# Biases of the first experts added by VectorE, turned rows copied a quad ahead, mask rows loaded by group, two scatters a step in the last group

## The reference

```python
x = layernorm(x + state_space_layer(x))
# first experts: 8 experts of hidden size 512, the best 2 for each token
out = 0.5 * gelu(flat @ shared_W + shared_b)
for e in range(8):
    h = gelu(flat @ W1[e] + b1[e])
    out = out + combine[:, e:e+1] * (h @ W2[e] + b2[e])
x = layernorm(x + layernorm(out) * gamma + beta)
# causal attention, 16 heads of size 8
x = layernorm(x + (softmax(mask(q k^T / sqrt(8))) v) @ Wo + bo)
# second experts: 64 experts, the best 4 for each token, 128 slots for each expert
x = layernorm(x + routed(x, router_w, w1, w2))
```

## Time and profile before

| what | value |
|---|---|
| median of three runs | 1650.65 us (1644.73 to 1650.91) |
| the profiled execution | 1646.96 us, its span 1645.1 us |
| busy share PE, DVE, ACT, POOL | 81%, 73%, 56%, 57% |
| mean granted clock of TensorE | 0.892 of full speed |
| first experts, projections, attention with routing | 259, 38 and 607 us |

### The profile page before, as it was taken

One profiled execution on the slowest core, in us unless ns is written; L12 is line 12 of the kernel. 1 busy time (PEld: TensorE's weight loads), 2 busy tenths in 40 slices (PEclk: granted clock), 3 DMA queues, 4 the chain that ended last, 5 costly groups with the idle time before them and its releaser, 6 DMA issues. The chain is left out here.

```text
span 1645.1 us, 25186 instructions
## 1 busy us (share of the span) xinstructions
PE 1332.7 (81%) x7232; PEld 716.4 (44%) x7235; DVE 1200.2 (73%) x2215; ACT 916.3 (56%) x1728; POOL 943.3 (57%) x779
## 2 busy tenths in 40 slices
PE   6848888888888989999926999999999998812756
PEld 2313333333333358898913244443343343212743
DVE  6999999999999554224477988889889886260325
ACT  5746666665666554456555076675666566601423
POOL 2478899988998117360756021214563654874773
PEclk9879899999999988999957599999999999955867
DMA  2019100000000025787728211211321114301317
GB/s 70 0 59 345 56 0 0 0 0 0 0 0 0 1 61 141 205 240 199 208 55 256 60 32 37 56 31 31 83 55 35 50 35 106 60 10 47 106 51 257
DMA packets 123041, 124.87 MB, mean 76 GB/s; under 512 B 31182, under 2 KB 97979, under 8 KB 120304
## 3 DMA queue, kind: packets, MB, share of 16 engines
q1 hardware_dynamic: 101032, 99.70, 21.8%
q0 software_dynamic: 10240, 15.79, 3.3%
q10 hardware_dynamic: 11656, 8.00, 1.6%
HBM read 78.52 MB, written 50.91 MB: 79 GB/s over the span
## 5 line engine op out<-in xcount | busy, mean ns | idle before, releaser
L2106 DVE TENSOR_REDUCE t_negm<-t_ps 128x1 f32<-128x512 f32 (+4 forms) x624 | 370.0, 642 | 56.7 <-PE t_ps L2374 35.2
L2083 ACT ACTIVATE t_PT<-t_ps_s 128x1024 f32<-128x1024 f32 (+3 forms) x384 | 292.1, 811 | 203.6 <-PE t_ps_s L2393 202.6
L493 POOL TENSOR_TENSOR s_HC<-s_H,X 128x1024 f32<-128x1024 f32 x128 | 307.0, 2416 | 40.3 <-DVE s_H L614 30.1
L658 PE MATMUL ps_y<-s_HC,ident 128*128 128x512 f32 x512 | 270.5, 655 | 19.8 <-POOL s_HC L493 17.9
L2011 POOL TENSOR_SCALAR_AFFINE_SELECT t_PT<-t_PT 128x512 f32<-128x512 f32 x128 | 82.7, 646 | 276.7 <-ACT t_PT L2083 276.2
L2374 PE MATMUL t_ps<-heads 96*128 96x512 bf16 (+3 forms) x640 | 201.3, 341 | 9.4 <-DVE t_negm L2106 7.6
L2393 PE MATMUL t_ps_s<-heads 96*128 96x512 bf16 (+3 forms) x768 | 181.0, 329 | 3.7 <-ACT t_PT L2083 2.1
L2408 PE MATMUL t_ps_c<-t_PT,t_VG 128*32 128x512 f32 (+3 forms) x1536 | 164.7, 502 | 1.7 <-ACT t_CT L2039 1.1
L554 ACT ACTIVATE s_dA<-m_DT,s_A 128x512 f32 (+1 forms) x192 | 127.4, 711 | 60.3 <-DVE s_H L614 59.4
L658 PEld LDWEIGHTS ps_y<-s_HC,ident 128*128 128x128 f32 x512 | 98.4, 204 | 124.1 <-issue 69.9
L1995 POOL DMA_INDIRECT slots<-X,t_idx_s x128 | 127.3, 994 | 34.9 <-issue 34.2
(11 more groups left out here) (347 smaller groups left out, 2367.2 us busy)
## 6 DMA issues: line engine op xcount, KB each, us to landing
f_w<-in_W_dram SPq DMA_DIRECT2D x93, 256.0 KB, 5.2
heads<-token_expert_rows SPq DMA_DIRECT2D x8, 1024.0 KB, 9.6
token_expert_rows<-X SPq DMA_DIRECT2D x42, 192.0 KB, 2.6
heads<-q_parts SPq DMA_DIRECT2D x42, 192.0 KB
heads<-k_parts SPq DMA_DIRECT2D x14, 576.0 KB
expert_rows<-X SPq DMA_DIRECT2D x27, 192.0 KB, 2.5
f_XS<-expert_rows SPq DMA_DIRECT2D x19, 256.0 KB
expert_rows_out<-f_YB ACTq DMA_DIRECT2D x19, 256.0 KB, 3.6
```

The lines of the kernel that those rows point to most:

```text
L493: nc.gpsimd.tensor_tensor(HC[:, g % RING], H[:, g % RING], row_wide(C_sb[:, g % RING, :], 2), ALU.mult).then_inc(s_hc, 2)
L658: nc.tensor.matmul(ps_y[c][:], ident[:], HC[:, g % RING, c, :], start=g == 0, stop=g == N - 1, skip_group_check=True).then_inc(s_y, 1)
L2083: nc.scalar.activation(PT[:, n % RP, 2 * p:2 * p + 2, 0:wd], src, ACT.Exp, scale=DK ** -0.5).then_inc(s_exp, 1)
L2106: nc.vector.tensor_reduce(out, ps_1[use % BANKS1][:, 0:h * width].rearrange("p (h k) -> p h k", h=h), AX.X, ALU.max, negate=True).then_inc ...
```

## The change

It has four edits. (1) The biases no longer go through TensorE. `b2` is spread to all partitions by one DMA (`b2_rows`), and `out_copy` becomes one addition for each block, with the expert's number read into a VectorE register first. The tables `comb`, `combT`, `b2big` and their work go; `ACC` is only halved (`halved`). (2) `rows_copy` is issued two quads ahead, just before `out_copy(q)`, instead of one quad ahead right behind `out_copy(q - 1)`. (3) The mask rows of group 0 are loaded at the top, those of groups 1 to 3 behind the stores of batches 0 to 2. (4) In group 15 up to two scatters follow each block.

```diff
-            nc.gpsimd.memset(b2big[:], 0.0).then_inc(s_z, 1)
-            sp.wait_ge(s_z, 1)
-            for t in range(NT // 2):
-                sp.dma_start(b2big[t * E0:(t + 1) * E0, t, :], io["b2"]).then_inc(s_b2, 16)
+            sp.dma_start(b2_rows[:].rearrange("p e n -> p (e n)"),
+                         io["b2"].rearrange("(a e) n -> a (e n)", a=1).broadcast_to([P, E0 * P])).then_inc(s_b2, 16)
...
-            def biases(i):
-                dve.wait_ge(s_b2m, i + 1)
+            def halved(i):
                 dve.wait_ge(s_gelu, i + 1)
                 part = ACC[:, i * PER:(i + 1) * PER, :].rearrange("p t n -> p (t n)")
-                nc.vector.scalar_tensor_tensor(out=part, in0=part, scalar=0.5, in1=ps_r[:], op0=ALU.mult, op1=ALU.add).then_inc(s_a0, 1)
+                nc.vector.tensor_scalar(part, part, 0.5, None, ALU.mult).then_inc(s_a0, 1)
...
             def out_copy(q):
                 dve.wait_ge(s_y, FIRSTB[q + 1])
...
-                cols = QUADS[q][2] * P
-                nc.vector.tensor_copy(YB[:, q % RY].rearrange("p a n -> p (a n)")[:, 0:cols], ps_y[q % 2][:, 0:cols]).then_inc(s_yc, 1)
+                for a in range(QUADS[q][2]):
+                    k = FIRSTB[q] + a
+                    e = dve.value_load(eid[0:1, k:k + 1], min_val=0, max_val=E0 - 1)
+                    b2_e = b2_rows[:, bass.ds(e, 1), :].rearrange("p a n -> p (a n)")
+                    last = nc.vector.tensor_tensor(YB[:, q % RY, a, :], ps_y[q % 2][:, a * P:(a + 1) * P], b2_e, ALU.add)
+                last.then_inc(s_yc, 1)
...
             rows_copy(0)
+            rows_copy(1)
             for q in range(NQ):
-                if q + 1 < NQ:
-                    rows_copy(q + 1)
                 if q == 0:
                     shares()
-                elif q == 1:
-                    turned_shares()
-                elif q < 2 + NCH // 2:
-                    biases(2 * q - 4)
-                    biases(2 * q - 3)
+                elif 2 <= q < 2 + NCH // 2:
+                    halved(2 * q - 4)
+                    halved(2 * q - 3)
...
+                if q + 2 < NQ:
+                    rows_copy(q + 2)
                 out_copy(q)
...
-            def b2_sum(i):
-                cols = b2big[:, (i % 4) * PER:(i % 4 + 1) * PER, :].rearrange("p t n -> p (t n)")
-                nc.tensor.matmul(ps_r[:], combT[:, i // 4, :], cols, start=True, stop=True).then_inc(s_b2m, 1)
...
-            for g in range(NG):
+            def mask(g):
                 for x, own_rows in enumerate((Q[g], K[g])):
                     sp.dma_start(own_rows[MASK_AT:P].rearrange("r j t -> r (j t)"), keep["mask_rows"][x]).then_inc(keep["s_mr"], 16)
+            mask(0)
...
+                if b + 1 < NG:
+                    mask(b + 1)
...
-                    if gi * NB + n >= (NG * (sent // (QTR * TOPK) + 1) + SCATTER[0]) * NB + SCATTER[1]:
-                        scatter(sent)
-                        sent += 1
+                    for _ in range(2 if gi + 1 == TG else 1):
+                        if gi * NB + n >= (NG * (sent // (QTR * TOPK) + 1) + SCATTER[0]) * NB + SCATTER[1]:
+                            scatter(sent)
+                            sent += 1
```

More of the change, by code:

```diff
@@ L913, in ffn @@
         sh_b = sb("sh_b", [P, P])
-        b2big = sb("b2big", [P, NT // 2, P])
+        b2_rows = sb("b2_rows", [P, E0, P])
         gamma = sb("gamma", [P, P])
@@ L923, in ffn @@
         wt = sb("wt", [P, 3, NT])
-        comb = sb("comb", [P, NT, E0])
-        combT = sb("combT", [P, 2, P])
         trif = sb("trif", [P, P])
@@ L967, in ffn @@
         s_w2 = sem("w2_loaded")
-        s_w, s_b2, s_z, s_k, s_lg, s_sh, s_tr = (sem(n) for n in (
-            "weights", "b2_loaded", "b2_zeroed", "constants", "logits", "shared", "x_turned"))
+        s_w, s_b2, s_k, s_lg, s_sh, s_tr = (sem(n) for n in (
+            "weights", "b2_loaded", "constants", "logits", "shared", "x_turned"))
         s_l, s_gelu, s_x1t, s_rt, s_d, s_exp, s_m, s_rk = (sem(n) for n in (
             "logits_copied", "shared_gelu", "x_token_major", "route", "difference", "gate_exp", "mask", "ranks"))
-        s_ix, s_ei, s_cb, s_ct, s_ctc, s_b2m, s_a0 = (sem(n) for n in (
-            "slots", "block_experts", "comb", "comb_t", "comb_t_copied", "b2_sum", "acc_begun"))
+        s_ix, s_ei, s_a0 = (sem(n) for n in ("slots", "block_experts", "acc_begun"))
         s_sc = keep["s_dispatched"]
@@ L1266, in shares @@
                 link(nc.vector.tensor_tensor(wt[:, 2, :], wt[:, 2, :], wt[:, 1, :], ALU.mult))
-                for r in range(2):
-                    also(nc.vector.tensor_tensor(oh[:, r], oh[:, r], wide(wt[:, 1 + r, :], E0), ALU.mult))
-                dve.wait_ge(s_rt, n)
-                nc.vector.tensor_tensor(comb[:], oh[:, 0], oh[:, 1], ALU.add).then_inc(s_cb, 1)
-            def turned_shares():
-                for h in range(2):
-                    dve.wait_ge(s_ct, 2)
-                    nc.vector.tensor_copy(combT[:, h, :], ps_r[:, h * P:(h + 1) * P]).then_inc(s_ctc, 1)
-            def biases(i):
-                dve.wait_ge(s_b2m, i + 1)
+            def halved(i):
                 dve.wait_ge(s_gelu, i + 1)
                 part = ACC[:, i * PER:(i + 1) * PER, :].rearrange("p t n -> p (t n)")
-                nc.vector.scalar_tensor_tensor(out=part, in0=part, scalar=0.5, in1=ps_r[:], op0=ALU.mult, op1=ALU.add).then_inc(s_a0, 1)
+                nc.vector.tensor_scalar(part, part, 0.5, None, ALU.mult).then_inc(s_a0, 1)
             m = 0
@@ L1296, in out_copy @@
                     dve.wait_ge(s_ys[q % RY], 16 * turns(q - RY, RY))
-                cols = QUADS[q][2] * P
-                nc.vector.tensor_copy(YB[:, q % RY].rearrange("p a n -> p (a n)")[:, 0:cols], ps_y[q % 2][:, 0:cols]).then_inc(s_yc, 1)
+                if q == 0:
+                    dve.wait_ge(s_b2, 16)
+                    dve.wait_ge(s_ei, 1)
+                elif q == GQ[1][0]:
+                    dve.wait_ge(s_ei, 2)
+                for a in range(QUADS[q][2]):
[4 more added lines that the diff above has]
+                last.then_inc(s_yc, 1)
             def mark(ins):
@@ L1477, in _ @@
                     ranks(1)
-            def comb_turned():
-                pe.wait_ge(s_cb, 1)
-                for h in range(2):
-                    nc.tensor.transpose(ps_r[:, h * P:(h + 1) * P], comb[:, h * 16:(h + 1) * 16, :].rearrange("p t e -> p (t e)"), ident[:]).then_inc(s_ct, 1)
-            def b2_sum(i):
-                pe.wait_ge(s_b2, 16 * NT // 2)
-                pe.wait_ge(s_ctc, 2)
-                if i:
-                    pe.wait_ge(s_a0, i)
-                cols = b2big[:, (i % 4) * PER:(i % 4 + 1) * PER, :].rearrange("p t n -> p (t n)")
-                nc.tensor.matmul(ps_r[:], combT[:, i // 4, :], cols, start=True, stop=True).then_inc(s_b2m, 1)
             def turn(q):
@@ L1546, in _ @@
                 down(k)
-                q, nth = QOF[k], k - FIRSTB[QOF[k]]
-                if q == 1 and nth == 0:
-                    comb_turned()
-                elif 2 <= q < 2 + NCH // 2 and nth < 2:
-                    b2_sum(2 * q - 4 + nth)
             pe.wait_ge(s_xc, NQ)
```

## The result

The changed kernel takes 1671.71 us in the median of four runs (1667.31 to 1675.44), the kernel before 1648.70 beside it: a ratio of 1.0134, 95% interval 1.0108 to 1.0161, that is 22 us slower (18 to 27). 1667 was forecast, in a range of 1656 to 1673. The profiled execution took 1669.09 us, its span is 1667.3: 22.2 more than before where the sum said 17.7.

A forecast was written before the change was run, and what follows sets the result against it. TensorE was taken to bound the first experts' blocks, GpSimd's scatters or what feeds them the late stretch. First experts +3.2, mask rows -0.5, scatters +15.0 make +17.7 us on 1648.8: 1666.5, say 1667, range 1656 to 1673.

The forecast's parts named there:

- the mask term: Projections: fewer mask loads ahead let the first batch's stores land sooner, and the moved loads land in time; -0.5 us.
- C: Output copies: register loads and additions run strictly in turn, 4.24 us a quad; total +21.6, 1670.5 us; chance 0.12.
- F: Attention's first product waits for the last mask pair, +5 in place of -0.5; total +23, 1672 us; chance 0.05.
- Scatters: Group 15: added scatters delay the last select 13.2 us, the last batch's scatters 11.9; TensorE's slow clock adds 3.1: +15.0 us.
- Rival D: Group 15: the second scatter costs the selects nothing, scatters start 1.3 us earlier; total +1.4, 1650.2 us; chance 0.05.
- E: Behind group 15's selects TensorE keeps the full clock; total +14.6, 1663.5 us; chance 0.15.
- B: Output copies: VectorE's register loads are nearly free, 1.16 us a quad; total +7.7, 1656.5 us; chance 0.16.
- TensorE -7.1: First experts: eight bias products and the turned tables leave TensorE, taking 7.1 us off it.
- Both roots +4.1: First experts: quad 11's extra work starts 2.07 us later, and this lateness adds fully at each of two roots: +4.1 us.
- Store of quad 15 +2.0: First experts: GpSimd's gather of the second group starts behind this store, later by three blocks' additions: +2.0 us.
- Last two copies +4.7: First experts' end: the back-to-back output copies take 3.37 + 2.60 us instead of 1.25, delaying both chains: +4.7 us.
- Copying rows ahead: First experts: copying turned rows a quad ahead only removes 0.61 us ahead of quad 11's extra work.

The follow-up runs named there:

- nothing behind the third batch: Kernel before, mask rows of groups 0 and 1 at the top, group 2 behind the first batch's stores, group 3 behind the second's; ratio 1.0022.
- SyncE's order changed: Against the kernel with edits 1 and 2: SyncE issues quad 5's weights ahead of quad 6's rows; 1.0020 of the kernel before.
- the kernel without loads: Edits 1 and 2, but each quad's output copy is one addition of the bias table's first rows, without register loads or choice by expert; ratio 0.9968.

## Why the prediction was right, and where only its sum was

The forecast's sign, its range and its largest term held. The stage of first experts came out near its sum by luck, since its errors cancel, and the mask term had the wrong sign. Of the 4.5 us by which the trace exceeds the sum, the mask rows alone are 5.0; the other differences cancel. By the time alone, 1671.7, rivals C (1670.5) and F (1672) fit better than the forecast, whose own span ended at 1670. It is the traces that decide between them.

**Scatters: +15.0 forecast, +15.3 and +15.1 in the two traces.** The last select is 13.2 us later, as summed from 1.28 us a scatter. The rest is mostly the price of the slow clock (3.1 forecast). From the last product to the first transposes behind the norm are 13.51 us instead of 10.62: +2.9, at a granted clock of 0.50 from 1454 to 1459 us and 0.55 from 1459 to 1464. One part of that sum was misread: the turned rows are eight transposes and not four (1.97 us instead of 1.09, +0.9 where 0.45 was summed), and the last product gave +0.2 instead of 0.4. Another 0.8 us, which the sum hadn't, pass between the last note (done at 1483.38) and the scatter that it releases (1484.21). From the last select to the last batch's first scatter are 30.17 us; before they were 28.06, of which the backlog took 1.6: 30.17 less 26.5 gives the same +3.7. Rival D falls by the 3.09 us between selects, E by the clock; B and C fall by the 0.75 us between additions, which are neither 0.29 nor 1.06. The clock fell in the 5.69 us of idling ahead of the first of the four products. The Trainium skill's "TensorE: Matmul & The Clock Gate", section "HAM oscillation — how this bites in real kernels", says that short bursts between waits fall to the slow clock. The trace agrees.

**Mask rows: -0.5 forecast, +4.5 by the traces and +3.5 timed.** The step that failed is that a load which lands in 6.9 us in the median and stands 9 us ahead of its use is in time. It took the latency of loads at the top for that of loads among the stores, and did not ask what the DMA engines were doing. With edit 3 alone such loads took up to 13.1 us to land. Rival F had the size, 5, and attention's first product did wait for the last pair; but with nothing behind the third batch the time stays, so that wait is not the cause. The price is the DMA engines' work, moved from an idle stretch into a full one.

**First experts: +3.2 forecast, +3.5 timed.** Means of the traces from the stage's first scatter on, six with neither edit 1 nor 2, three with edits 1, 2 and loads in turn (the changed kernel, edits 1 and 2 alone, SyncE's order changed):

| stretch | before | edits 1, 2 | moved | forecast |
|---|---|---|---|---|
| first scatter to the turn of quad 6 | 71.2 | 70.8 | -0.5 | -5.4 |
| to the turn of quad 9 | 23.3 | 22.4 | -0.9 | -1.7 |
| to the first root | 32.7 | 34.7 | +2.0 | +2.07 |
| to the second root | 10.9 | 10.7 | -0.2 | +2.07 |
| to the second group's gather | 29.7 | 31.4 | +1.7 | +2.0 |
| to the third group's gather | 43.6 | 45.9 | +2.3 | +4.7 |
| to the end of the stage | 33.3 | 33.2 | -0.2 | 0 |
| sum | 244.7 | 249.0 | +4.3 | +3.7 |

Between traces of one column a row varies by up to 2.6 us, and the sums lie at 242.7 to 246.2 and at 246.2 to 251.7, so the small differences are rough. The forecast's -0.5 for the earlier routing is not in the table; the first scatter itself came at 616.7 us in the mean of the seven traces with edit 1 and at 616.6 in the seven without, so that term is nothing.

- *TensorE -7.1 failed: about 1.4 came.* I had read TensorE's busy row at 710 to 720 us and taken it for the whole row of blocks. The eight bias products stand at 664 to 696, six of them (with the turned tables 5.4 us) ahead of quad 6's turn. Before the change SyncE could load that quad's rows only at 681.45, after 3.5 us of waiting for GpSimd's scatters, and TensorE turned them at 687.37, not far behind. What sets the time there is GpSimd's row of scatters, so a faster TensorE waits instead, first for weights queued behind those rows, or, with the queue turned round, for the rows themselves.
- *Both roots +4.1: 1.8 by the traces.* The price of a quad's additions was right (0.75 us apart, 0.77 forecast), and the first root comes 2.0 us later, as summed. But for the second root the step "any lateness adds fully" counted it on top of the copy's own wait. VectorE used the 3.53 us that it had idled, and from root to root it waits for no other engine.
- *Store of quad 15 +2.0: 1.7.* The size fits, the cause isn't shown: the kernel without loads has 32.4 us in the same stretch, more than the 31.4 with them.
- *Last two copies +4.7: 2.3.* Seven additions took 5.1 us where 6.0 was summed (and the two copies took 1.32, not 1.25), and the store of the first of the two quads leaves 2.6 us ahead of the second: the next gather starts 2.8 us after the last addition, 3.9 before the change.
- *Copying rows ahead "is this -0.61 and nothing else" failed.* Without edit 1 nothing measured speaks against it. With it, edit 2 saves some 12 us that TensorE would else wait for turned rows. The forecast named the right result because both edits were made; the sentence would have misled anyone who took only the first.

What is left of the 22.2 us: from attention's first product to group 15 lie 508.9 to 514.0 us in the fourteen traces, 510.8 before and 513.8 after, without regard to the edits. In part it is seen: at the end of group 14 TensorE was granted 0.83 of its clock in ten microseconds of the kernel before (1385 to 1395 us) and 0.66 in the same ten of the changed one (1394.3 to 1404.3), and VectorE's wait for a product there was 8.90 instead of 7.44 us. What makes the clock fall there in some runs was not tried.

The Trainium skill's "DMA: Bandwidth & Descriptors", section "Latency and other measured facts", gives a tensor load a floor of some 600 ns. Here VectorE's 85 loads last 0.30 us in the median, and a load with its checks shows as 0.46 us of idling between two additions, 0.75 from start to start with the addition. The measurement decides.

## What to carry to other kernels

Read the busy row of the engine that is relieved in the very stretch where its work goes away, and ask what it would catch up with: here the blocks with the bias products ran just behind another engine's row of scatters. Look at the DMA engines' share before a transfer is moved later, since an idle stretch ahead of a full one is capacity that can't be got back. An instruction in front of an output copy is judged by what stands behind it in the same queue and when that is wanted, not by the idle time ahead of it; and register loads belong where the engine idles, well ahead of the wait.

## What the runs showed of the hardware

- A register load on VectorE with its check and address costs 0.46 us of idling each, in turn with additions of 0.29. Four loads done ahead let four additions follow in 0.88 us.
- The 16 DMA engines can be the bound of a stage in which each of four compute engines is busy for some two thirds: a share of 0.85 to 1.03 in the projections. Some seven more idle microseconds of theirs at its start cost 4.5 at its end.
- Traces of one and the same stage, with no edit in it, differ by 3.5 us in 245 (242.7 to 246.2) and by 5 in 511. A term below that needs several traces or timed runs.
